# One product of 192 columns for each head's scores in the first cross attention of a two-layer gated block

## The reference, cut to what matters

```
q = (queries @ wq_w + wq_b).reshape(B, S, H, DK).transpose(0, 2, 1, 3)
k_proj = keys @ wk_w + wk_b
k_ext = jnp.concatenate([k_proj, jnp.broadcast_to(mk, (B, MEM, H * DK))], axis=1)
scores = jnp.einsum('bhsd,bhtd->bhst', q, k) / jnp.sqrt(jnp.float32(DK))
attn = jax.nn.softmax(scores, axis=-1)
out = jnp.einsum('bhst,bhtd->bhsd', attn, v)
```

## Time and profile before

| what | us |
|---|---|
| median of 3 runs | 4331.2 (4321.15 to 4336.77) |
| profiled execution | 4334.09 |
| span of its trace | 4332.1 |
| TensorE busy | 4143.6 (96%) |
| VectorE busy | 3517.0 (81%) |
| GpSimd busy | 2862.6 (66%) |
| ScalarE busy | 2835.9 (65%) |

### The profile page before, as it was taken

How to read it: one execution, slowest core, us unless ns; L and a number is a source line. 1 busy time by engine, 2 the same in 40 slices (tenths; PEclk the granted TensorE clock), 3 DMA queues, 4 the chain that set the end, 5 groups by cost and what they waited for, 6 DMA issues and landing times.

```text
span 4332.1 us, 149193 instructions
## 1 busy us (share of the span) xinstructions
PE 4143.6 (96%) x51751; PEld 2895.4 (67%) x51751; DVE 3517.0 (81%) x7208; ACT 2835.9 (65%) x6406; POOL 2862.6 (66%) x3633
## 2 busy tenths in 40 slices
PE   5999998999999999999999999999999999788799
PEld 4777775666666666666666666666666666566665
DVE  4666667899889888889888998889989998577566
ACT  2555555777777777777777777777777777455322
POOL 2333336888778887788877887788878887455200
PEclk9999999999999999999999999999999999778699
DMA  2000010000000001000010001000010000000000
GB/s 88 6 7 6 7 30 22 8 10 9 24 20 10 7 10 32 13 7 10 18 26 9 9 8 30 15 8 9 9 35 10 8 9 6 19 12 12 2 10 10
DMA packets 162228, 64.86 MB, mean 15 GB/s; under 512 B 121556, under 2 KB 156128, under 8 KB 162016
## 3 DMA queue, kind: packets, MB, share of 16 engines
q1 hardware_dynamic: 162016, 62.05, 5.7%
HBM read 26.54 MB, written 2.10 MB: 7 GB/s over the span
## 4 chain that ended last, share of the span: by engine, by line
PE 87%; issue 5%; DVE 3%; POOL 3%; SPq 1%; ACT 1%; DMA 0%; DVEq 0%; POOLq 0%; ACTq 0%
PE pj L1543 15%; PE pp L1698 9%; PE pj L1550 8%; PE po L1635 6%; PE po L1618 5%; PE sc L1589 5%; PE pp L1573 4%; PE pp L1602 4%; PE turn L1573 4%; PE pp L1674 3%; PE pj L1481 3%; PE pp L1439 3%; PE po L1454 2%; PE sc L1833 2%; PE pj L1473 2%
## 5 line engine op out<-in xcount | busy, mean ns | idle before, releaser
L1543 PE MATMUL pj<-wqkv,xcT 128*128 128x512 f32 x1536 | 807.5, 608 | 30.4 <-DVE big L1109 18.7
L633 POOL TENSOR_TENSOR qn<-qn,big 128x512 f32<-128x512 f32 x384 | 489.5, 1275 | 285.7 <-DVE big L1109 285.7
L794 ACT ACTIVATE big<-pj 128x512 f32<-128x512 f32 x768 | 465.1, 606 | 159.8 <-PE pj L1543 147.1
L1109 DVE TENSOR_TENSOR big<-pj,ropes 128x512 f32<-128x512 f32 x768 | 522.2, 680 | 0.0
L1115 DVE TENSOR_REDUCE ss<-big 128x8 f32<-128x512 f32 x768 | 515.5, 672 | 3.7 <-ACT big L794 3.7
L633 POOL TENSOR_TENSOR big<-big 128x512 f32<-128x512 f32 x384 | 485.2, 1274 | 18.5 <-DVE big L1109 18.4
L1698 PEld LDWEIGHTS pp<-wo,oT 128*128 128x128 f32 x3072 | 357.3, 191 | 156.1 <-issue 84.2
L628 POOL TENSOR_TENSOR e<-e,rc 128x512 f32<-128x512 f32 x384 | 400.2, 1042 | 63.3 <-DVE rc L1139 63.2
L622 POOL TENSOR_TENSOR qn<-qn,ny 128x512 f32<-128x512 f32 x384 | 396.3, 1043 | 7.5
L622 POOL TENSOR_TENSOR big<-big,ny 128x512 f32<-128x512 f32 x384 | 396.3, 1043 | 7.5
L1698 PE MATMUL pp<-wo,oT 128*128 128x128 f32 x3072 | 393.9, 281 | 1.6 <-ACT oT L817 1.2
(11 more groups left out here) (324 smaller groups left out, 9902.9 us busy)
## 6 DMA issues: line engine op xcount, KB each, us to landing
wqkv<-in_L_ffn_Wqkv SPq DMA_DIRECT2D x18, 512.0 KB, 3.5
xsd<-Y SPq DMA_DIRECT2D x192, 32.0 KB
xsd<-Y SPq DMA_DIRECT2D x384, 15.8 KB
xsf<-Y SPq DMA_DIRECT2D x96, 64.0 KB
xsf<-Y SPq DMA_DIRECT2D x192, 31.5 KB
xsx<-Y SPq DMA_DIRECT2D x64, 64.0 KB, 1.8
xsx<-CT SPq DMA_DIRECT2D x64, 64.0 KB, 1.9
wo<-in_L_ffn_Wo SPq DMA_DIRECT2D x6, 512.0 KB, 4.4
```

Of the source, the lines that this page charges most:

```text
L633: nc.gpsimd.tensor_tensor(U[a.par][i], U[a.par][i], t2b[i % 2], ALU.add).then_inc(sem("d_add"), 1)
L794: nc.scalar.activation(sqb[i % 2], pj[i % 2][:, :], ACT.Square).then_inc(sem("d_sq"), 1)
L1109: nc.vector.tensor_tensor(t2v, swapped, sin, ALU.mult).then_inc(sem("d_r"), 1)
L1543: mm(pj[i % 2][:, :], xcT[:, a.par, :], wqkv[:, i * 512:i * 512 + 512], start=True, stop=True).then_inc(sem("d_ch"), 1)
```

## The change

The keys of a tile are now kept with the memory keys beside them. For half of the heads (four head pairs, in two groups `u` of two) and for each batch there is a row of 384 columns: 128 of the memory for head pair a2 = 0, the 64 own ones of a2 = 0, the 64 own ones of a2 = 1, 128 of the memory for a2 = 1. There are two such slots. Slot 0 lies in `wqkv`, slot 1 in two new tensors `kbuf`; `kT` becomes a part of `kbuf[0]`. `scores(s)` is now eight products of 192 columns, one for each head and batch, in place of four of 128 and eight of 64. VectorE writes the own keys with two instructions of 256 columns in place of one of 512. ScalarE copies the memory keys into both slots, for both batches, once before the stage: eight copies of 512 columns in place of two. SyncE waits, before it loads the layer-0 weights into `wqkv`, until the scores of tile 30, the last that uses slot 0, are done. To make room `xsf` and `hT` lose a second half (their slot index is always 0).

```diff
-        kT = sb("kT", [P, HP, P])
+        kbuf = [sb("kbuf%d" % i, [P, 12 * P]) for i in range(2)]
+        kT = kbuf[0][:, 0:HP * P].rearrange("p (h t) -> p h t", h=HP)
...
-        xsf = sb("xsf", [P, 2, FT, D])
+        xsf = sb("xsf", [P, 1, FT, D])
...
-        hT = sb("hT", [P, 2, 3, FT * P])
+        hT = sb("hT", [P, 1, 3, FT * P])
...
-        x_k = [kT, bq[:, 2048:3072].rearrange("p (h t) -> p h t", h=HP)]
+        x_k = [[wqkv[:, 12 * P * i:12 * P * i + 12 * P] for i in range(2)], [kbuf[i][:, :] for i in range(2)]]
+
+        def key_rows(v):
+
+            return v.rearrange("p (u b c) -> p u b c", b=BT, c=3 * P)
...
             sp.wait_ge(sem("edge"), 1)
+            past(sp, "x_s", 4 * (NT - 1))
             for part in ("q", "scales", "k", "v", "o"):
                 attention_weights(0, part)
...
                 act.wait_ge(sem("mk_T"), i + 1)
-                nc.scalar.copy(mkT[:, 4 * i:4 * i + 4, :].rearrange("p h m -> p (h m)"), pt_[:, :]).then_inc(sem("mk_c"), 1)
+                for slot in range(2):
+                    for bb in range(BT):
+                        mem = key_rows(x_k[slot][i])[:, :, bb, :].rearrange("p u (z m) -> p u z m", m=MEM)[:, :, 0::2, :]
+                        last = nc.scalar.copy(mem, pt_[:, :].rearrange("p (u a m) -> p u a m", a=2, m=MEM))
+                last.then_inc(sem("mk_c"), 1)
...
                         elif what == "k":
-                            nc.vector.tensor_tensor(x_k[a.par][:, hs, :], pj[0][:, :].rearrange("p (h t) -> p h t", h=4), bc(kb[:, hs], P), ALU.add).then_inc(sem("x_ev"), 1)
+                            for u in range(2):
+                                own = key_rows(x_k[a.par][i])[:, u, :, P:2 * P].rearrange("p b (a t) -> p a b t", a=2)
+                                src = pj[0][:, 2 * P * u:2 * P * u + 2 * P].rearrange("p (a b t) -> p a b t", a=2, b=BT)
+                                bias = bc(kb[:, 4 * i + 2 * u:4 * i + 2 * u + 2], BT)
+                                last = nc.vector.tensor_tensor(own, src, bc(bias, S), ALU.add)
+                            last.then_inc(sem("x_ev"), 1)
...
                         for a2 in range(2):
                             for par in range(2):
                                 r = slice(par * 64, par * 64 + 64)
-                                c0 = a2 * 256
-                                mm(x_sc[s % 2][par][:, c0:c0 + MEM], x_q[b.par][r, 2 * s + a2, :], mkT[r, 2 * s + a2, :], start=True, stop=True)
-                        for a2 in range(2):
-                            for par in range(2):
-                                r = slice(par * 64, par * 64 + 64)
-                                c0 = MEM + a2 * S
                                 for bb in range(BT):
                                     q = slice(bb * 64, bb * 64 + 64)
-                                    last = mm(x_sc[s % 2][par][q, c0:c0 + S], x_q[b.par][r, 2 * s + a2, q], x_k[b.par][r, 2 * s + a2, q], start=True, stop=True)
+                                    keys = key_rows(x_k[b.par][s // 2])[r, s % 2, bb, a2 * 192:a2 * 192 + 192]
+                                    last = mm(x_sc[s % 2][par][q, a2 * 192:a2 * 192 + 192], x_q[b.par][r, 2 * s + a2, q], keys, start=True, stop=True)
                         last.then_inc(sem("x_s"), 1)
```

## The result

| | median us | lowest to highest | runs |
|---|---|---|---|
| before | 4325.5 | 4316.7 to 4336.77 | 6 |
| after | 4300.0 | 4292.91 to 4305.51 | 6 |

The ratio is 0.9942, with a 95% interval of 0.993 to 0.9955: faster by 0.58%. The forecast was 4311 in a range of 4299 to 4325. Against the profiled execution of before (4334.1) the forecast saving was 20.2 us; the profiled execution of after took 4305.5, 28.6 less. By the medians of six runs each the saving is 25.5. So the direction is right, and some 5 to 8 us came from a place that the prediction does not speak of.

What follows compares the result with a forecast made beforehand. TensorE was taken to bound stage 1. 23.8 us from 99 shorter products, less 0.5 (xT), 0.2 (key evacuation) and 2.9 (copies), gave 20.2 saved, so 4311 from a median of 4331.2; range 4299 to 4325.

Steps and rivals of the forecast that it cites:

- The bound: Stage 1 goes at TensorE's pace, so time taken from TensorE counts; the pass shrinks from about 19.65 to about 18.9 us.
- The product: Each scores(s) on TensorE falls from 1.04 to 0.80 us, reckoned from a 512-column product of the same form in cross attention.
- Both rivals that doubted four quarters at a time: Scores product: slower rounds, 0.94 to 1.00 us, 4325 to 4331 (chance 0.08); quarters taking turns, 1.46 us, 4386 (chance 0.04).
- `scores(0)` given back: At the pass start its 0.24 us becomes longer waiting of the q chunk on VectorE's L1071, in 29 passes.
- The rival in which this chain moves too: VectorE's chain at the pass start moves as well, all 128 products count: 7 us more saved, 4304; chance 0.05.
- Stage 1's sum: 99 products x 0.24 = 23.8 us, less 0.5, 0.2 and 2.9: 20.2 us saved.
- xT waits: After scores(1), xT waits for VectorE's copy in every other pass: 0.04 us lost in 15 passes, 0.5 us.
- The eight copies: ScalarE's memory-key copies before stage 1, eight in place of two, are bare: 2.9 us lost.
- The key evacuation: VectorE's two instructions in stage 1 take 0.75 us, 0.06 more, hidden except for 0.2 us in the fill passes.
- SyncE's wait: Layer-0 weights, loaded later at the end of stage 1, still arrive in time for stage 2, covered by at least 9 us.
- Behind stage 1: Stage 2 and what follows have no term in the sum of 20.2 us saved.
- The second rival: More waits in stage 1 swallow the saving: 4318 if scores(1) is given back too, 4325 with another; chance 0.07.

Runs made afterwards that it cites:

- experiment 2: The kernel before with its four memory products of a scores(s) split per batch into eight, so all sixteen have one form; old layout: 4290.8 us, ratio 0.991.
- the repeats: The kernel before and the changed kernel, each run again unchanged: 4332.6 us (ratio 1.0007) and 4306.0 us (ratio 0.9932).
- experiments 10 and 11: Kernel before and changed kernel, each without five of six rope table instructions at the five layer changes (not complete kernels): 4306.6 us and 4282.2 us.
- kernel 6: The kernel before with memory products split per batch and the chunk of q waiting for tmp, not the residual sum: 4283.0 us, ratio 0.989.
- kernel 5: The kernel before with only the wait of the chunk of q moved from the residual sum to tmp: 4317.6 us, ratio 0.9979.

## Why the prediction was right, and where it was not

**The bound, right.** TensorE set stage 1, and its time came back nearly in full: 0.70 a pass.

**The product, right.** 0.80 said, 0.81 measured, by the sum from the 512-column row. The reason given, no change of form in the middle, is shown by experiment 2, which removes only that. Both rivals that doubted four quarters at a time fell: 0.94 or more and 1.46 were their products. The factor of 3.07 that the Trainium skill gives, on the page "TensorE: Matmul & The Clock Gate" in "Measured speedup vs the span model", for four tiles of 32 rows, would have made it 1.00 by the prediction's estimate. The trace of these quarters of 64 rows does not show it.

**`scores(0)` given back, right.** The chunk starts 0.05 after L1087 ends, and its wait on the weight load went from 0.23 to 0.46. The rival in which this chain moves too fell.

**Stage 1's sum, mis-sized by 2 us.** 20.2 said, 18.1 measured. From the first input turn to stage 2 it was 648.7 and is 627.6, 21.1 less, where 23.1 were said (22.2 less in the repeats: 649.8 and 627.6). Two terms were too good. A product saves 0.226 (1.037 to 0.811), not 0.24, which is 1.4 us over 99. xT waits more than was said: `scores(1)` takes 0.91 to it in every other pass, so 0.10 and not 0.04 is lost, 1.5 us in 15 passes and not 0.5, since xT starts 0.15 after the copy's end (327.68 to 327.83) and not 0.06. Against them stands a repeated pass that is 0.70 shorter, where three products of 0.226 and that wait give 0.63; where the 0.07 come from no run shows. The eight copies ahead of it cost 43.96 - 40.93 = 3.03 where 2.9 were said. The first input turn waits for the last of them:

```profile
43.96 0.69 PE L1508 MATMUL pp<-K,xsx 128*128 128x128 f32 x2 [2.14 <-ACT kbuf L751]
```

**The key evacuation and SyncE's wait, right.** 0.76 for 0.75 and hidden; the weights issued 49.6 us later and in time. The second rival, more waits that swallow the gain, fell but for the 0.10 of xT's copy in every other pass.

**Behind stage 1, wrong.** The sum took all that follows stage 1 as unchanged. It fell by 10.3 us in the profiled executions, 8.8 of them in stage 2; by the medians, 25.5 less the 18.1 of stage 2's start, it is some 7. The step that failed is the silent one: that code which is not edited takes the time it took. Five times, once at each layer change, TensorE stands 3.3 us for VectorE, whose small instructions wait for GpSimd one by one, and its clock then is at the lower level for 3.4 us or more; in the changed kernel the stands are 2.5 to 2.9. How these fall beside each other depends on a microsecond. The row was on the page before: L1543's idle time, 18.7 us ended by DVE big L1109. I had read it as fixed.

The forecast's middle missed by 11 us, and that its range held the result, by 1 us, is luck in part. 5.7 of the 11 are the start: the forecast stood on 4331.2, the median of three runs of before, and that of six is 4325.5. The other 5.3 are the larger saving, 25.5 for 20.2.

## What to carry to other kernels

Products that use the array in another form than their neighbours cost about 0.2 us here for one change of form less (1.04 to 0.83 in experiment 2); giving a mixed group one form may need a loop only, no new layout, so try that first. Read a wait on the weight-load row as well as on the matmul, and ask which instruction of a chain really frees the bank. Where an edit moves everything ahead of a stage, look at that stage's largest stands: if small VectorE instructions with two SBUF inputs run there beside GpSimd, the time is not fixed, and they may be worth as much as the edit: leaving them out took 25 us off stage 2 and 21 off the median here. A complete kernel that moves them off the path was not tried. And compare medians before you explain a difference of 10 us between two traces.

## What was not expected of the hardware

- Sixteen records over four quarters cost 0.81 in one order and 0.83 in the order that uses each quarter twice in a row, and 0.83 as thirty-two shorter ones.
- A 32-column VectorE instruction took 0.18 with GpSimd idle and 1.04 to 1.08 beside it.
- In the kernel before a stand of 3.3 us was followed by 3.4 us at the lower of the two clock levels at four changes of five, and by 6.8 at the fifth. Without the tables it never fell there (0 us in experiments 10 and 11). Shorter ones were followed by it at some changes: two pieces of 0.94 and 1.18 us in kernel 6, at its second, brought 3.4 us of it, where 2.93 in one piece in kernel 5, at its first, brought none.
- 96 instructions at the start of TensorE's program, run while it waited for loads, went with a stage 2, 650 us later, that was 8.5 us shorter in one kernel and 5.8 longer in the other, in one trace each, where the repeat of an unchanged kernel moved it by 3.0 and 5.3.
